# A fused attention and mixture-of-experts kernel: its set-up loop rewritten, with output strips of 32 rows, other engines and another order of loads

## What is computed

```python
x1 = _layernorm(x)                       # of the first layer
q  = (Q @ Wq + bq).transpose(0, 2, 1)    # Q is x normalised; Wq is 256 x 16
k_ = (K @ Wq + bq).transpose(0, 2, 1)    # K and V are the context
corr = real(ifft(fft(q) * conj(fft(k_)))).mean(axis=(0, 1))
W_topk, I_topk = top_k(corr, 12); W_topk = softmax(W_topk)
R3 = sum over the 12 of w * roll(v, -shift)
attn = R @ Wout + bout
```

## Time and profile before

| | |
|---|---|
| median of 3 runs | 1632.08 us (1622.58 to 1641.44) |
| the profiled execution | 1633.12 us, span 1631.4 us |
| PE, DVE busy over the span | 1299.2 us (80%), 1074.0 us (66%) |
| ACT, POOL busy over the span | 979.0 us (60%), 722.7 us (44%) |
| mean granted clock of PE | 0.889 of 2.4 GHz |
| DMA | 216.83 MB, mean 133 GB/s |

### The profile page before, as it was taken

How to read it: one execution, slowest core, us unless ns; L and a number is a source line. 1 busy time by engine, 2 the same in 40 slices (tenths; PEclk the granted TensorE clock), 3 DMA queues, 4 the chain that set the end, 5 groups by cost and what they waited for, 6 DMA issues and landing times. The chain is left out here.

```text
span 1631.4 us, 29997 instructions
## 1 busy us (share of the span) xinstructions
PE 1299.2 (80%) x9486; PEld 889.7 (55%) x9486; DVE 1074.0 (66%) x3044; ACT 979.0 (60%) x1878; POOL 722.7 (44%) x886
## 2 busy tenths in 40 slices
PE   5952375688888898888888888888888898878865
PEld 4742353455666566655665666556665565545533
DVE  4744433457777777786778677867776677676754
ACT  1311221356777677776777677767776767676774
POOL 2313424236444644464446544554445444444331
PEclk9985586789999999999999899989998999998996
DMA  8762345444444444454444444444444443333200
GB/s 273 223 230 61 117 143 170 140 125 126 140 141 133 154 135 138 138 157 138 138 138 151 144 138 138 144 135 138 135 125 128 128 134 119 99 99 113 67 8 13
DMA packets 169173, 216.83 MB, mean 133 GB/s; under 512 B 19002, under 2 KB 157628, under 8 KB 162492
## 3 DMA queue, kind: packets, MB, share of 16 engines
q1 hardware_dynamic: 162876, 198.15, 39.1%
q0 software_dynamic: 6144, 16.79, 3.0%
HBM read 133.33 MB, written 79.43 MB: 130 GB/s over the span
## 5 line engine op out<-in xcount | busy, mean ns | idle before, releaser
L1110 DVE TENSOR_REDUCE mx<-mx_pair 128x4 f32<-128x1024 f32 x256 | 312.5, 1221 | 79.4 <-PE mx_pair L1370 55.2
L692 POOL TENSOR_TENSOR hid<-hid,t 128x256 f32<-128x256 f32 x256 | 195.0, 771 | 251.8 <-DVE t L1156 251.1
L848 ACT ACTIVATE pt<-ex_pair 128x1024 f32<-128x1024 f32 x256 | 261.6, 1022 | 11.5 <-PE ex_pair L1315 11.5
L1370 PE MATMUL mx_pair<-ks,qs 62*128 62x256 f32 x1024 | 144.8, 361 | 85.4 <-DVE mx L1110 61.8
L1370 PEld LDWEIGHTS mx_pair<-ks,qs 62*128 62x128 f32 x1024 | 93.1, 213 | 170.8 <-DVE mx L1110 121.5
L905 DVE BATCH_NORM_STATS2 bn<-x 128x6 f32<-128x256 f32 x192 | 72.0, 417 | 165.5 <-POOL x L696 139.9
L1331 PE MATMUL bank<-pt,va 128*32 128x256 f32 x2048 | 178.7, 423 | 0.0
L877 ACT ACTIVATE hid<-bank 128x256 f32<-128x256 f32 x256 | 98.9, 386 | 127.9 <-PE bank L1341 117.8
L1315 PE MATMUL ex_pair<-qs,ks 64*128 64x256 f32 x1024 | 138.7, 352 | 40.4 <-ACT pt L848 33.9
L1315 PEld LDWEIGHTS ex_pair<-qs,ks 64*128 64x128 f32 x1024 | 83.7, 202 | 116.4 <-issue 52.2
L1156 DVE SCALAR_TENSOR_TENSOR t<-th,bank 128x256 f32<-128x256 f32 x256 | 106.7, 417 | 44.7 <-ACT th L883 36.6
(11 more groups left out here) (213 smaller groups left out, 2805.8 us busy)
## 6 DMA issues: line engine op xcount, KB each, us to landing
ks<-ksplit_d SPq DMA_DIRECT2D x192, 128.0 KB
qs<-qsplit_d SPq DMA_DIRECT2D x192, 128.0 KB, 3.1
ys_d<-ys SPq DMA_DIRECT2D x56, 256.0 KB
xs<-xs_d SPq DMA_DIRECT2D x24, 512.0 KB
x<-in_x SPq DMA_DIRECT2D x32, 256.0 KB, 3.9
va<-in_ctxT SPq DMA_DIRECT2D x32, 256.0 KB, 3.6
xl<-in_x SPq DMA_DIRECT2D x32, 256.0 KB
x_d<-xl SPq DMA_DIRECT2D x32, 256.0 KB, 5.5
```

The source lines that it names most:

```text
L692: pool.tensor_tensor(part_, part_, t1[:, c % 2], ALU.mult).then_inc(hid_made, 1)
L848: act.activation(pt[:, slot:slot + 2].rearrange("p i a c -> p (i a c)"), ex_pair[:, :], ACT.Exp).then_inc(ex_made[u % 2], 1)
L1110: dve.tensor_reduce(mx[:, t].rearrange("p (r g j) -> p r g j", r=2, j=2)[:, :, g], mx_pair[:, :].rearrange("p (r j s) -> p r j s", r=2, j= ...
L1370: ins = pe.matmul(shared_bank(job, r)[:, j * S:(j + 1) * S], qs[par][rows, 2 * g + j, t * P:(t + 1) * P], ks[par][rows, 2 * g + j, :], sta ...
```

## The change

- PE: the products of a batch go into a strip of 32 rows of the bank (four strips; batch b has strip b mod 4, and the two batches of a group that share a strip take its upper and lower 16 rows through the window of `z`). The k product runs one batch ahead of the q product, so neighbours in the queue are in different strips. q and k have two banks each, by turns of group. Each group's Gram products come inside the loop, half a group later; only the last group's stand behind it. The mean of the weights is taken ahead of them.
- ACT applies the normalisation (two activations a batch, with scale and bias), beside its evacuation. POOL makes the bias with one more multiply. DVE keeps the statistics, with three sets of buffers, and the weights' sums stand between them, after batches 18, 22 and 26.
- SP: the x ring has six tiles (two are in `x4`). The early loads stand between the first tiles. The weights go one a batch from batch 8 on; `ew` behind the diagonal reads, the first zero fill behind the circulant read, `eb_r` and the second fill with the fourth batch's load in the pipeline. Their users wait for `first_ld` and `late_ld`.
- DVE rounds and casts the weights ahead of the row of lags; POOL fills `ks`, `va` and `qs` as their space comes free.

```diff
+            def early_x(b):
+                if b >= XA:
+                    sp.wait_ge(a_xn, b - XA + 1)
+                sp.dma_start(xa_at(b % XA), x[b:b + 1].rearrange("o (t p) d -> (o p) t d", p=P)).then_inc(xa_ld[b % XA], 16)
...
+            def early_ctx(b):
+                if b >= CA:
+                    sp.wait_ge(a_k, b - CA + 1)
+                sp.dma_start(ca_at(b % CA), ctxT[b:b + 1].rearrange("o (k p) s -> (o p) k s", p=P)).then_inc(ca_ld[b % CA], 16)
+            def weights():
+                for src, dst in ((wgT, raw_w[0]), (wuT, raw_w[1])):
+                    sp.dma_start(dst.rearrange("p (k n) -> p k n", k=KT), src.rearrange("(k p) n -> p k n", p=P)).then_inc(raw_ld, 16)
+                    yield
...
+                for dst, src in ((rw, rwT), (by_head[0], wqT), (by_head[1], wkT), (wv, wvT), (wo, woT)):
+                    sp.dma_start(dst[:], src.rearrange("(k p) n -> p k n", p=P)).then_inc(w_ld, 16)
+                    yield
...
+                for dst, src, n in ((bv_r, bv, D), (bo_r, bo, D), (rb_r, rb, NE), (bout_r, bout, D)):
+                    sp.dma_start(dst[:], bass.AP(src.tensor, 0, [[0, P], [1, n]])).then_inc(w_ld, 16)
+                    yield
...
+            def zero_rows(i):
+                sp.dma_start(xs_d[i].rearrange("(i p) d -> p i d", p=P),
+                             xn[:, 0].unsqueeze(1).to_broadcast([P, TILES, D])).then_inc((first_ld, late_ld)[i], 16)
...
+            early_x(0)
+            sp.dma_start(wq_raw, wq0.rearrange("(k p) n -> p k n", p=P)).then_inc(early_ld, 16)
             sp.dma_start(bq0_c, bass.AP(bq0.tensor, 0, [[0, GROUP], [1, L0_DH], [1, 1]])).then_inc(early_ld, 16)
-            sp.dma_start(wq_raw, wq0.rearrange("(k p) n -> p k n", p=P)).then_inc(early_ld, 16)
+            early_x(1)
+            early_ctx(0)
+            early_x(2)
+            early_ctx(1)
             sp.dma_start(wout_s, wout_r.rearrange("(k p) n -> p k n", p=P)).then_inc(early_ld, 16)
...
+            rest = weights()
+            for b in range(2, NB):
+                if b + 1 < NB:
+                    early_x(b + 1)
+                early_ctx(b)
+                if b >= GROUP:
+                    next(rest, None)
+            for _ in rest:
+                pass
...
+            sp.dma_start(ew[:], ewT.rearrange("(k p) n -> p k n", p=P)).then_inc(first_ld, 16)
...
+            zero_rows(0)
...
+                    if b.n == FOUR - 1:
+                        sp.dma_start(eb_r[:], bass.AP(eb.tensor, 0, [[0, P], [1, NE * D]])).then_inc(late_ld, 16)
+                        zero_rows(1)
...
+            def rstd(b):
+                i = b % 3
                 pool.wait_ge(a_var, b + 1)
-                pool.tensor_tensor(rs[:, j], ve[:, j], mhalf[:], ALU.pow).then_inc(a_rstd, 1)
...
+                pool.tensor_tensor(rs[:, i], ve[:, i], mhalf[:], ALU.pow).then_inc(a_pow, 1)
+                pool.wait_ge(a_pow, b + 1)
+                pool.tensor_tensor(nm[:, i], mneg[:, i], rs[:, i], ALU.mult).then_inc(a_rstd, 1)
...
+            pool.tensor_copy(ks[1][:], nm_rows[:, 2:3].unsqueeze(2).to_broadcast([P, H // 2, S])).then_inc(stacks_ready, 1)
+            pool.wait_ge(a_k, NB)
             pool.memset(va[:], 1.0).then_inc(stacks_ready, 1)
+            for i in range(2):
+                pool.wait_ge(tern, 10 + i)
+                pool.memset(qs[i][:].bitcast(F32), 1.0).then_inc(stacks_ready, 1)
...
+            pool.tensor_copy(ks[0][:], nm_rows[:, 2:3].unsqueeze(2).to_broadcast([P, H // 2, S])).then_inc(stacks_ready, 1)
...
+            def apply(b):
+                i = b % 3
+                act.wait_ge(a_rstd, b + 1)
+                if b >= 2:
+                    act.wait_ge(a_xnT, b - 1)
+                for t in range(T):
+                    ins = act.activation(xna[:, b % 2, t], xa_at(b % XA)[:, t], ACT.Identity, bias=nm[:, i, t:t + 1],
+                                         scale=rs[:, i, t:t + 1])
+                ins.then_inc(a_xn, 1)
...
+                    act.wait_ge(a_q, b - 1)
...
+                act.wait_ge(a_q, GROUP * (g + 1))
+                act.wait_ge(a_k, GROUP * (g + 1))
...
+            apply(0)
+            for b in range(NB):
+                if b + 1 < NB:
+                    apply(b + 1)
+                evacuate(b)
+                if b % GROUP == 1 and b > 1:
+                    group_out(b // GROUP - 1)
+            group_out(NG - 1)
...
+                        if b.n == 0:
+                            act.wait_ge(first_ld, 16 * 2)
+                            act.wait_ge(late_ld, 16 * 2)
...
+            for b in range(NB):
+                dve.wait_ge(xa_ld[b % XA], 16 * (b // XA + 1))
+                if b >= 3:
+                    dve.wait_ge(a_xn, b - 2)
+                stats(xa_at(b % XA), b % 3, a_stats, a_var, b, lambda k: 4 * b + k)
+                if b in WABS_AFTER:
+                    i = WABS_AFTER.index(b)
+                    if i == 0:
+                        dve.wait_ge(raw_ld, 16 * N_RAW)
+                    ins = dve.tensor_reduce(wabs[:, i:i + 1], raw_w[i], AX_X, ALU.add, apply_absolute_value=True)
+                    if i == 2:
+                        ins.then_inc(tern, 1)
...
+            for i in range(3):
+                dve.wait_ge(tern, 4 + i)
+                dve.tensor_scalar(raw_w[i], raw_w[i], 1.0, MAGIC, ALU.min, ALU.add).then_inc(tern, 1)
+            for i, w in enumerate((wg, wu, wd)):
+                dve.wait_ge(tern, 7 + i)
+                dve.tensor_scalar(w[:].rearrange("p k n -> p (k n)"), raw_w[i], MAGIC, None, ALU.subtract).then_inc(tern, 1)
...
             dve.wait_ge(lagstep, L_CORR)
...
+                            dve.wait_ge(late_ld, 16 * 2)
...
+            def product(b, banks, k, src):
+                strip, late = b % STRIPS, b % GROUP // STRIPS
+                at = strip * (P // STRIPS)
+                w = z[:, k, P - L0_DH - late * L0_DH:P + L0_DH - late * L0_DH]
+                return pe.matmul(banks[b // GROUP % 2][at:at + P // STRIPS, 0:S], w, src, start=(late == 0 and k == 0),
+                                 stop=(late == 1 and k == KT - 1))
...
+            def products(b):
+                if b + 1 < NB:
+                    pe.wait_ge(ca_ld[(b + 1) % CA], 16 * ((b + 1) // CA + 1))
+                if b % GROUP == GROUP - 1 and b >= 2 * GROUP - 1:
+                    pe.wait_ge(a_grp, b // GROUP)
+                if b >= 0:
+                    pe.wait_ge(a_xt, b + 1)
...
+                    if b >= 0:
+                        q = product(b, q0_banks, k, xta[:, b % 2, k])
+                    if b + 1 < NB:
+                        kp = product(b + 1, k0_banks, k, ca_at((b + 1) % CA)[:, k])
+                if b >= 0:
+                    q.then_inc(a_q, 1)
+                if b + 1 < NB:
+                    kp.then_inc(a_k, 1)
...
+            transposes(0)
+            products(-1)
+            for b in range(1, NB):
+                transposes(b)
+                products(b - 1)
+                if b % GROUP == 4 and b > GROUP:
+                    gram(b // GROUP - 1)
+            products(NB - 1)
+            pe.wait_ge(tern, 1)
+            pe.matmul(bank[0][:, 0:3], ones[:], wabs[:], start=True, stop=True).then_inc(wsum, 1)
+            gram(NG - 1).then_inc(lagstep, 1)
```

201 lines of the change are left out of this document (49 added, 152 removed).

## The result

The changed kernel takes 1622.8 us (median of 20 runs, 1610.51 to 1632.08), the kernel before beside it 1637.39 (20 runs, 1622.58 to 1642.75): ratio 0.9917, 95% interval 0.9894 to 0.9941. The profiled executions say the same: span 1616.1 against 1631.4, 15.3 less.

The account below looks back on a forecast made before the run. PE bounded the projections, latencies the chain behind. Projections to 70, plus 35.2 for the chain and 0.5 for the pipeline's start, gave 105.7 against 146.44: 40.7 us off 1633.1, so 1592 us (range 1582 to 1606).

Parts of the forecast that it names:

- the first fill: Chain: behind the circulant read its 2 MB take 5.2 us of DMA, while the next store waits 10 us or more.
- Step 1: Projection loop: strips overlap, four products take 1.00 us, and PE needs 1.43 us a batch with transposes, against 2.16.
- the drain rival: Projection loop: array empties at each shape change, 0.34 or 0.68 us a batch instead of 0.14; time 1594, chance 0.15.
- step 5: End of projections to first pipeline load: 35.2 us against 48.41, with six of eight Gram matmuls moved into the loop.
- my 70: End of projections, at the start of the last group copy: 70 us against 98.03, bounds 66 and 75.
- The rival of no overlap: Projection loop: strips run in turn, PE needs 2.30 us a batch, projections end at 87.8; time 1610, chance 0.08.
- a clock at half throughout: Projection loop: PE at half clock needs 2.86 us a batch, projections end at 106; time 1628, chance 0.03.
- Step 2: Normalisation on ACT in the loop: 1.57 to 1.69 us a batch, with ACT leading and DMA close.
- Step 3: Start of the loop: first normalisation at 13.2 us, and the old 12.26 us hole gone.
- Step 4: Loop loads: 19 input tiles issued by about 20.0 us, a hole of 3 to 5 us, projections end at 68.7.
- Step 6: Pipeline start: second fill and eb_r with batch 3's load delay batch 4's tile by 0.5 us, bounds 0 and 10.
- The step from set-up to time: Pipeline after its first load: the remaining 1485 us stay the same, so a shorter set-up shifts the end equally.

Follow-up runs that it names:

- e4: Changed kernel with all weights loaded behind the last input tile and their sums behind the loop: 1621.16 us.
- e8: Changed kernel with the three 1 MB weight loads issued right behind the first tiles instead of at batches 8, 9 and 10: 1614.09 us.
- e7: Changed kernel with rings of 8 x tiles and 5 ctx tiles instead of 6 and 4: 1628.74 us.
- e10: Changed kernel with large loads early, earlier start, matrices behind Gram reads, POOL fills late, zero fills behind circulant read, extra PE matmuls, rings 7 and 5: ratio 0.985.
- e5: Changed kernel with POOL's three fills of qs and ks waiting until the row of lags is written: 1613.57 us.
- e3: Changed kernel with eb_r behind ew and the second zero fill right behind the first, both ahead of the pipeline: 1617.61 us, ratio 0.9881 to before.
- e1: Kernel before with only its two zero fills moved behind the circulant read: 1621.83 us, ratio 0.992.
- e2: Changed kernel with the strips undone, each product writing all 128 rows again: 1631.61 us, ratio 0.9971 to before.
- e6: Changed kernel with 10 extra PE matmuls ahead of the column sums and 22 ahead of the products behind the circulant read: 1623.62 us.

## Why the prediction was wrong

The direction, the overlap of strips and the first fill were right, the size was not. In the profiles 25.4 us of the forecast 40.7 are missing: 18.5 in the loop (88.55 instead of 70, the q copy), 4.6 in the chain (39.77 instead of 35.2), 3.4 in the pipeline's start (3.9 instead of 0.5), less 1.1 behind it, which I take for chance.

The forecast of 1592 counts from one execution of 1633.1; beside the change the kernel before took 1637.4, so 4.7 of the 30.8 us between 1592 and 1622.8 are the base.

- **Step 1, strips: the overlap right, PE's sum too small.** Two strips overlap. The four products take 0.98 (forecast 1.00); the transposes in front take 0.59 where they took 0.43, so the changes of shape cost 0.28 a batch instead of 0.14, nearer to the 0.34 of the drain rival; whether the array drains there the rows don't say. I also took the Gram products out of step 5 without adding them to the loop, a term of 2.9 us put at nothing. PE's own work came to 57.0 us (e4) and not 45.8: from the first transposes at 15.0 it alone would end at 72.0, 2.0 past my 70, and PE, not ACT, is the slowest engine. The rival of no overlap falls, and so does that of a clock at half throughout: it was at 0.50 only for a part of the loop (0.50 to 0.67 from 36 to 52 us), which cost 4.9 us of PE time (61.9 against 57.0).
- **Step 2, ACT: its own time right.** 1.46 to 1.57 a batch where nothing is late; but it does not lead, PE's 1.57 does.
- **Step 3, start: right.** First normalisation at 13.79, forecast 13.2.
- **Step 4, DMA: the step that failed.** I assumed 19 input tiles issued by 20 us. It was 12, because the seventh x tile waits behind the fifth ctx tile in SP's queue, and that for the first k product; the DMA engines lost the time from 12 to 20. I had asked which engine is slowest per batch and taken the rings as able to absorb the rest, instead of following SP's own queue through its waits. The burst I had priced at 3 to 5 us of hole; ACT waited 16.8 in all. Of the 18.5 us that are missing in the loop 16.5 lie here: PE stood 11.6, and its half clock in the burst cost 4.9. e8 shows that moving the three large loads from the burst into the hole gives 8.9 us; e4 that the weights cost 12.2 in all; e7 that depth gives 2.5. The earlier start, deeper rings and matrices out of the loop gave 5.5 more (e10). There PE is busy for 57.4 of the 66.4 us from its first product to the q copy at 74.1, so what is left above PE's own work is 8.9 us of waits, most of them for tiles; whether DMA volume or the order of loads sets these I did not separate.
- **Step 5, chain.** Gram, store, reads and sums came as forecast: 11.3 instead of 11.8. The 23.4 behind them became 28.5. 2.76 of the 5.05 is POOL: I moved DVE's rounding ahead of the row, noted that POOL's fills follow it and called them 10 us ahead of need, and did not ask what they do to DVE meanwhile. e5 shows it. Another 2.0 is PE's clock in the last products, and 0.3 is spread over the rest.
- **Step 6, second fill: mechanism half right.** 3.9 came, within the bounds of 0 and 10 but far from the 0.5 that I took. I followed batch 4's x tile through the DMA backlog, and missed that its load waits for batch 2's stash to land, which SP issues just behind the 3 MB. e3 gives 3.0 of the 3.9 back.
- **The step from set-up to time: right.** Behind the first scatter the length is the same program and the same time, 1446.8 against 1447.9; that they agree to 1.1 is partly luck, for the same stretch spreads over 18.7 us in the table. A better mark than the first load would have been the first scatter.

Why the clock was low in the last products is open. In the executions that have a trace the granted clock rose from 0.50 either 3.3 to 4.4 us after PE's first product behind the circulant read (before, e1, e4, e5, e7, e8; last products 3.7 to 3.8 us) or 8.7 to 9.4 us after it (changed, e2, e3, e6; 5.8 to 6.1 us). The rows of e5, with the first product at 110.75, are

```profile
114.00:116.00 2.00, 1.25 (x5) 0.67 (x4) 0.00 (x0) 1.43 (x4) 0.00 (x0) 0.85 0.55 194
116.00:118.00 2.00, 2.00 (x11) 1.74 (x11) 0.00 (x0) 1.33 (x3) 0.00 (x0) 1.00 0.00 0
```

and those of the changed kernel, with the first product at 113.60,

```profile
117.00:119.00 2.00, 1.25 (x3) 0.78 (x3) 0.00 (x0) 1.58 (x4) 0.00 (x0) 0.50 0.49 172
119.00:121.00 2.00, 2.00 (x6) 1.53 (x6) 0.00 (x0) 1.16 (x3) 0.00 (x0) 0.50 0.00 0
```

PE does the same work in both. It is not DMA beside the products either, for e1 had a share of 1.09 beside them and took 3.7 us. Nor does PE's idle time ahead of them tell the two apart: it was 10.8 to 14.4 us in the first group, and 14.3 to 14.4 (5.3 in e6) in the second. It moves 2 us. Each kernel has one trace, so whether the same kernel does now one and now the other, and whether the change has a part in it, is not shown.

## What to carry to other kernels

Before a loop is priced by its slowest engine, follow the queue that issues its loads through its own waits: one tile that waits for a product holds back every load behind it, and time in which the DMA engines stand at the start is missing later (8.9 us here). Then add up everything that the slowest engine does in the loop, also what was moved into it. Price a large fill by what stands behind it in the queue and waits for landing, not by its bytes, and look for a place where nothing small follows. Work on POOL that is "early enough" is free only if DVE isn't on the path beside it.
